# One decoder layer on one core: scores' matrix laid out batch by batch, fillers in the early gaps, all instruction orders rewritten

## The reference, cut to what matters

```
x = layernorm(x + attn(x));  x = layernorm(x + xattn(x, ctx));  x = layernorm(x + ffn(x))

attn:  q, k = elu(x Wq + bq) + 1, elu(x Wk + bk) + 1;  v = x Wv + bv        (16 heads of 8)
       k = k / sqrt(sum(k*k) + 1e-6);  out = (q k^T) v per head, then Wo
       a layernorm of x + out, times gamma, plus beta
xattn: q = x Wq, k = ctx Wk, v = ctx Wv   (16 heads of 64);  softmax(q k^T / 8) v, then Wo
ffn:   fp4_linear(x, w) = quant_dequant(x) @ quant_dequant(w)^T
       h = silu(fp4_linear(x, gate)) * fp4_linear(x, up);  fp4_linear(h, down)
       quant_dequant: blocks of 16, scale = max|x|/6, nearest value of 0, .5, 1, 1.5, 2, 3, 4, 6
```

## Time and profile before

| what | us |
|---|---|
| median of 3 runs | 360.56 |
| the profiled execution: its own time | 362.69 |
| the profiled execution: its span | 360.9 |
| TensorE busy | 342.2 (95%) |
| VectorE busy | 307.8 (85%) |
| GpSimd busy | 271.8 (75%) |
| ScalarE busy | 256.0 (71%) |

### The profile page before, as it was taken

One profiled execution on the slowest core, in us unless ns is written; L12 is line 12 of the kernel. 1 busy time (PEld: TensorE's weight loads), 2 busy tenths in 40 slices (PEclk: granted clock), 3 DMA queues, 4 the chain that ended last, 5 costly groups with the idle time before them and its releaser, 6 DMA issues.

```text
span 360.9 us, 7621 instructions
## 1 busy us (share of the span) xinstructions
PE 342.2 (95%) x2319; PEld 288.1 (80%) x2319; DVE 307.8 (85%) x851; ACT 256.0 (71%) x533; POOL 271.8 (75%) x453
## 2 busy tenths in 40 slices
PE   6789999999999999999999999999999999989884
PEld 6588858787779979977799977888897888968763
DVE  1599986667799998988889988989999987999994
ACT  2678886776788685797857677877877767666543
POOL 3275779889978769798777578979979897794445
PEclk9899999999999999999999999999999999999999
DMA  7821100000100000111001000001000000001001
GB/s 233 290 62 31 39 8 16 0 16 2 46 29 2 1 2 0 45 32 31 0 2 40 7 1 17 15 3 29 2 1 17 1 16 15 4 15 31 0 23 37
DMA packets 13587, 10.46 MB, mean 29 GB/s; under 512 B 971, under 2 KB 12396, under 8 KB 13548
## 3 DMA queue, kind: packets, MB, share of 16 engines
q1 hardware_dynamic: 12540, 7.89, 7.2%
q10 hardware_dynamic: 1008, 2.10, 1.6%
HBM read 7.88 MB, written 2.10 MB: 28 GB/s over the span
## 4 chain that ended last, share of the span: by engine, by line
PE 52%; POOL 16%; issue 14%; DVE 11%; ACT 4%; DMA 1%; POOLq 0%; ACTq 0%; DVEq 0%
PE A L2880 11%; PE S L2850 8%; PE TP L2837 5%; PE TP L2868 5%; PE F L2904 4%; POOL pe L445 3%; PE A L2798 3%; PE A L2924 2%; PE S L2859 2%; POOL fold L439 2%; PE TP L2776 2%; POOL hv L455 2%; DVE smax L1838 2%; PE TP L2913 2%; DMA wqkT<-in_wk_t 1%
## 5 line engine op out<-in xcount | busy, mean ns | idle before, releaser
L445 POOL TENSOR_TENSOR pe<-pe,srec 128x1024 f32<-128x1024 f32 x32 | 60.8, 1905 | 5.0 <-DVE srec L1855 4.9
L2880 PEld LDWEIGHTS A<-wvoT,wqkT 128*128 128x128 f32 x480 | 56.1, 192 | 2.0 <-issue 1.2
L2880 PE MATMUL A<-wvoT,wqkT 128*128 128x128 f32 x480 | 57.3, 275 | 0.0
L2850 PE MATMUL S<-M,x1T 128*128 128x512 f32 x192 | 52.8, 410 | 0.7 <-DVE x1T L1737 0.7
L439 POOL TENSOR_TENSOR fold<-pe 128x512 f32<-128x512 f32 x32 | 42.1, 1314 | 12.6 <-ACT pe L1081 12.4
L2850 PEld LDWEIGHTS S<-M,x1T 128*128 128x128 f32 x192 | 34.0, 189 | 10.4 <-issue 1.8
L1838 DVE TENSOR_REDUCE smax<-S 128x16 fp32r<-128x1024 f32 x32 | 38.9, 1215 | 2.2 <-PE S L2850 2.2
L1086 ACT ACTIVATE wqkT<-TP 128x1024 f32<-128x1024 f32 x32 | 32.7, 1021 | 10.9 <-PE TP L2868 10.8
L1081 ACT ACTIVATE pe<-S 128x1024 f32<-128x1024 f32 x32 | 32.6, 1018 | 5.8 <-PE S L2859 5.6
L2868 PE MATMUL TP<-ident,pe 128*128 128x128 f32 x256 | 33.6, 274 | 0.5 <-ACT wqkT L1086 0.2
L2904 PE MATMUL F<-w_gu_r,xf_r 128*128 128x352 f32 x168 | 33.9, 337 | 0.1
(11 more groups left out here) (246 smaller groups left out, 914.6 us busy)
## 6 DMA issues: line engine op xcount, KB each, us to landing
xT<-in_x_t SPq DMA_DIRECT2D x16, 128.0 KB, 2.2
x_sb<-in_x SPq DMA_DIRECT2D x16, 128.0 KB, 2.2
out<-yf SPq DMA_DIRECT2D x15, 128.0 KB, 1.8
pe<-in_fw SPq DMA_DIRECT2D x1, 560.0 KB, 10.6
wqkT<-in_wq_t ACTq DMA_DIRECT2D x2, 256.0 KB, 4.8
wqkT<-in_wk_t ACTq DMA_DIRECT2D x2, 256.0 KB, 6.3
ctx_f<-in_ctx_t ACTq DMA_DIRECT2D x2, 256.0 KB, 7.4
wvoT<-in_wv_t ACTq DMA_DIRECT2D x1, 512.0 KB, 8.9
```

The lines of the kernel that those rows point to most:

```text
L445: ge.tensor_tensor(w, w, spread(srec[n % NFO][:, :], HX, R), ALU.mult).then_inc(pn_made, 1)
L2850: last = te.matmul(S[:, half * BANK:half * BANK + BANK], part(x1T[b % 2][:, left, :], t), M[:, g % 2, right, HC * half:HC * half + HC, b % ...
L2880: last = te.matmul(part(A2, t), pT[n % 2][:, j, :], vo[b % 2][:, j, :], start=(j == 0 and b not in SUM_ON_PE), stop=(j == NJ - 1))
```

## The change

1. M becomes `[P, 2, 2, BG, HX, R]`: what `scores` reads is one run of 512 columns. ACT and DVE now read PSUM in runs of 64 columns (`m_by_batch`) and write four runs of 256.
2. Fillers: 5 before `g_product(0)`, 5 before `project_kv(1)`, 4 before `project_q(0)`, 4 before `kv_outer(0)`. Near the end 38 in nine places, where there were 24 in four.
3. The order of the calls is another one on all five engines. Functions and numbers of calls are the same.

```diff
-        M = sb("M", [P, 2, 2, HX, BG * R], FP32R)
+        M = sb("M", [P, 2, 2, BG, HX, R], FP32R)
+        def m_by_batch(g, q):
+            return M_BANKS[NQ * g + q][:, :].rearrange("p (h b r) -> p b h r", h=QH, b=BG)
         def m_part(g, q, part):
-            return M[:, g % 2, part, QH * q:QH * q + QH, :]
+            return M[:, g % 2, part, :, QH * q:QH * q + QH, :]
-                sc.activation(m_part(g, q, 0), m_bank(g, q), ACT.Copy).then_inc(m_high, 1)
+                sc.activation(m_part(g, q, 0), m_by_batch(g, q), ACT.Copy).then_inc(m_high, 1)
-                ve.tensor_tensor(m_part(g, q, 1), m_bank(g, q), m_part(g, q, 0).bitcast(FP32), ALU.subtract).then_inc(m_low, 1)
+                ve.tensor_tensor(m_part(g, q, 1), m_by_batch(g, q), m_part(g, q, 0).bitcast(FP32), ALU.subtract).then_inc(m_low, 1)
                     for half in range(2):
-                                         M[:, g % 2, right, HC * half:HC * half + HC, b % BG * R:b % BG * R + R],
+                                         M[:, g % 2, right, b % BG, HC * half:HC * half + HC, :],
...
             pe.wait_ge(const_made, 5)
+            keep_warm(A2, 5)
             g_product(0)
             project_kv(0)
             pe.wait_ge(fk_made, 1)
+            keep_warm(S0, 5)
             project_kv(1)
             g_product(1)
             pe.wait_ge(fk_made, 2)
+            keep_warm(S0, 4)
             project_q(0)
             pe.wait_ge(ky_made, 3)
+            keep_warm(S0, 4)
             kv_outer(0)
             kv_project(0)
             pe.wait_ge(fq_made, 1)
-            project_q(1)
+            project_kv(2)
             attn_out(0)
...
             project_kv(4)
-            pe.wait_ge(m_low, 5)
-            m_product(1, 3)
-            pe.wait_ge(m_low, 7)
-            x1_transpose(0)
-            pe.wait_ge(m_low, 6)
-            hw_product(1)
-            pe.wait_ge(fk_made, 5)
-            project_q(4)
             scores(0, 0)
             values(0)
+            pe.wait_ge(fk_made, 5)
+            project_q(4)
             scores_shift(0, 0)
-            pe.wait_ge(ky_made, 15)
-            kv_outer(3)
-            pe.wait_ge(fq_made, 5)
-            project_kv(5)
-            pe.wait_ge(pe_made, 1)
-            x1_transpose(1)
-            kv_project(3)
             pe.wait_ge(vo_kept, 1)
             values(1)
+            pe.wait_ge(pe_made, 1)
+            x1_transpose(1)
+            pe.wait_ge(m_low, 8)
+            weights_transpose(0)
+            pe.wait_ge(m_low, 8)
+            weights_transpose(1)
             pe.wait_ge(x1T_low, 2)
             scores(0, 1)
...
             xf_transpose(13)
             pe.wait_ge(hT_kept, 12)
+            pe.wait_ge(hT_kept, 12)
+            keep_warm(TP0, 8)
             p_transpose(15, 0)
...
             pe.wait_ge(yf_made, 13)
-            keep_warm(A2, 4)
+            pe.wait_ge(hg4_made, 14)
+            keep_warm(S0, 4)
+            down(13)
+            pe.wait_ge(yf_made, 14)
+            pe.wait_ge(hg4_made, 14)
+            keep_warm(S0, 2)
             tile_xf_transpose(15, 0)
-            pe.wait_ge(xfT_kept, 16)
-            down(13)
             pe.wait_ge(hg4_made, 15)
+            pe.wait_ge(hg4_made, 14)
+            keep_warm(S0, 5)
             tile_gate_up(15, 0)
```

More of the change, by code:

```diff
@@ L545, in _ @@
             shift_of("post", 0)
+            x_plus_rows(2)
+            k_norm(2)
+            minus_mean("attn", 1)
+            variance_eps("attn", 1)
+            rstd_of("attn", 1)
+            shift_of("attn", 1)
+            context_low(1)
             times_gamma(1)
@@ new lines, in _ @@
+            variance_eps("post", 8)
+            rstd_of("post", 8)
+            shift_of("post", 8)
+            k_norm(10)
+            variance_eps("attn", 9)
+            x_plus_rows(10)
+            minus_mean("ffn", 2)
+            minus_mean("attn", 9)
+            rstd_of("attn", 9)
+            shift_of("attn", 9)
+            h_dequantise(3)
+            times_gamma(9)
+            plus_x_beta(9)
+            fold_halves(7, 1)
+            probabilities(7, 0)
+            x_dequantise(5)
@@ L2067, in _ @@
+            k_miss(2, 1)
             aggregate("attn", 1)
[L2068 to L2071 removed]
             q_features(2)
             k_better(2, 1)
[L2074 removed]
             m_keep_low(1, 0)
+            m_keep_low(1, 1)
             keep_kvT(2)
[L2077 removed]
+            m_keep_low(1, 2)
             q_features(3)
+            weights_rounded_up()
             k_sums(3)
+            x1T_keep_low(0)
@@ L2370, in _ @@
+            xf_keep_low(5)
+            gated(4, 1)
+            h_max(4)
+            m_keep_low(3, 2)
+            score_reciprocals(7, 1)
+            ffn_residual(3)
+            score_max(8, 1)
+            score_sums(8, 0)
+            attn_residual(10)
+            statistics("attn", 10)
+            h_reciprocal(4)
+            x_max(6)
+            x_reciprocal(6)
+            h_scaled(4)
+            aggregate("attn", 10)
             statistics("ffn", 3)
-            aggregate("ffn", 3)
@@ L2586, in _ @@
+            score_sums(13, 0)
+            score_sums(13, 1)
+            score_reciprocals(13, 0)
+            score_reciprocals(13, 1)
+            statistics("cross", 12)
+            x_max(11)
+            aggregate("cross", 12)
+            x1T_keep_low(14)
+            gate_times(10, 0)
             attn_residual(15)
+            gated(10, 0)
             statistics("attn", 15)
             aggregate("attn", 15)
-            h_rounded_up(9)
-            h_rounded(9)
-            x_max(11)
+            score_max(14, 0)
@@ L2987, in _ @@
             m_product(0, 0)
-            pe.wait_ge(fq_made, 2)
-            project_kv(2)
             m_product(0, 1)
+            pe.wait_ge(fk_made, 3)
+            project_q(1)
             m_product(0, 2)
@@ L3116, in _ @@
             project_q(6)
-            pe.wait_ge(h_made, 1)
-            gate_up(0, 1)
-            pe.wait_ge(vo_kept, 5)
-            m_product(2, 0)
+            pe.wait_ge(pT_kept, 6)
+            values(4)
             pe.wait_ge(ky_made, 24)
```

2100 lines of the change are left out of this document (1029 added, 1071 removed).

## The result

The changed kernel takes 361.86 us (median of 7 executions, 361.46 to 362.25), the kernel before beside it 360.69 (7 executions). The ratio is 1.0027, interval 1.0017 to 1.0037: 1.2 us slower, where 1.2 us faster was forecast.

What follows compares the result with a forecast made beforehand. TensorE's work was taken to bind 71% of the span, with VectorE beside it early and VectorE alone in the tail. Terms +1.2 - 2.4 - 0.7 + 0.7 = -1.2 us took the 360.56 us median to 359.4, range 356.8 to 362.5.

Steps and rivals of the forecast that it cites:

- M batch by batch: nothing.: Scores' matmul: reading one run of 512 columns instead of runs of 64 gains nothing; at best 2.9 us less.
- Fillers at the start: +1.2 us.: Start, up to `m_product(0, 0)`: the added fillers lengthen the chain by 1.2 us; bounds 0 and +2.8.
- if the clock now holds: Start, at `project_kv(1)` and `g_product(1)`: full clock wins back 1.6 us, so `project_kv(1)` ends only 0.3 late.
- if the clock falls all the same: Start, upper bound +2.8 us: 5 fillers cost twice their time and the 1.6 us are not won.
- The offset: The sum: profiled execution 362.69 us becomes 361.5; the median is 2.13 lower, 360.56, so 359.4 us is predicted.
- Orders between 19.35 and 54: -2.4 us.: Up to 54 us: moved weights' steps and `k_norm(1)` win 2.4 of TensorE's 2.74 us idle time; bounds 2.74 and 0.
- Orders between 54 and 310: -0.7 us.: The middle: new orders win half of TensorE's 1.41 us idle time; bounds -1.41 and +1.4.
- The tail: +0.7 us.: Near the end: fillers before `tile_gate_up(15, 0)` and `tile_xf_transpose(15, 0)` cost 0.7 us, between 0 and 1.7.
- Slower: fillers behind their waits: Rival, at 11.7, 15.8 and 344 us: fillers behind waits lengthen the chain, 4.5 against 2.4 us; 362.7 us, chance 0.24.

Runs made afterwards that it cites:

- b_layout: The kernel before with nothing but M's layout changed: 360.84 us, ratio 0.9999 to the kernel before.
- a_no_start: The changed kernel without its 18 fillers at the start: 360.62 us, ratio 1.0000 to the kernel before.
- b_start: The kernel before with only the 18 start fillers added, behind their waits: 362.85 us, ratio 1.0057 to the kernel before.
- b_same: The kernel before, unchanged, run and profiled a second time: 360.73 us, ratio 1.0003.
- u_weights: New orders, fillers ahead of their waits, none before `g_product(0)` (357.87 us), with `weights_scaled` and `weights_rounded_up` put back to their old places: 361.48 us.
- f_wru: The kernel before with `weights_rounded_up` moved on VectorE to behind `x1T_keep_low(0)`: 361.47 us, ratio 1.0019 to the kernel before.
- f_dve2: As f_wru, with `weights_scaled` also moved, to behind `keep_kvT(1)`: 362.36 us, ratio 1.0041 to the kernel before.
- a_no_tail7: The changed kernel without the 7 fillers before `tile_xf_transpose(15, 0)` and `tile_gate_up(15, 0)`: 360.22 us, ratio 0.9986 to the kernel before.
- c_start_ahead: As a_no_tail7, with the fillers before `project_kv(1)`, `project_q(0)` and `kv_outer(0)` ahead of their waits: 360.97 us, ratio 0.9990 to the kernel before.
- c_none7: The changed kernel without the 18 start fillers and without the tail's 7: 360.74 us, ratio 0.9977 to the kernel before.

## Why the prediction was wrong, step by step

- **M batch by batch: nothing.** Right: 393 ns against 394, and b_layout at 0.9999.
- **Fillers at the start: +1.2 us.** This is the step that failed. Measured: 1.03 us to `project_kv(0)` and 1.52 behind it, 2.55 in all (after against a_no_start), and 2.0 in the old orders (b_start). The step had the parts right that follow their waits. It credited 1.6 us for "if the clock now holds", read from the earlier trace rows, and called the 5 before `g_product(0)` hidden behind the start at 9.11. In b_same `project_kv(0)` starts at 8.26 with no gap, so nothing hides them. The fall of the clock is common in the kernel before, but it costs far less than 1.6 us: 0.74 to `scores(8, 0)` in the execution of the forecast, 0.13 where it came at 16.4 us in b_layout, and nothing in the medians of the 120 executions. Low clock made single calls longer there; that the chain to the scores got longer by as much was taken without a reason. The 2.8 us that stood as the bound "if the clock falls all the same" is what came, without a fall.
- **The offset.** The sum was made against an execution of 362.69 us and carried over by a constant 2.13. But 1.6 of these were the late start of `project_kv(0)` and the 0.74 us behind it, the very things that the start's step had the fillers cure. The gain was booked against a median in which it had no place. That alone turns -1.2 into +0.4.
- **Orders between 19.35 and 54: -2.4 us.** The size was larger: -3.38 to `scores(8, 0)` (a_no_start against b_same), and the first scores came at 40.83 us, not at 42 to 43. That is more than the bound of 2.74, all the idle time from 19.35 to 54. Only 1.03 of the 3.38 is idle time; the step had no term for a shorter busy time of TensorE. The two steps did get short in their new places, and putting two steps of the weights back costs 3.6 us (u_weights), in which the shared port makes VectorE 1.1 us later. But in the old lists the same moves lose (f_wru, f_dve2). So each list is fitted to itself, and which share of the gain is the weights' steps' stays open.
- **Orders between 54 and 310: -0.7 us.** Nothing: 254.59 busy in both, and +0.38 from `scores(8, 0)` to the last `gate_up`, within the bounds.
- **The tail: +0.7 us.** Too small: 1.18 in the profile, in the upper half of its bounds. The busy VectorE covered none of the 5.
- **Rivals.** "Slower: fillers behind their waits" is the one that came true, with 2.55 + 1.18 = 3.7 us of its 4.5, against 3.4 - 0.4 = 3.0 brought by the orders in the profiles. It had a chance of 0.24. What spoke for it stood in the forecast's own rows: a profiled execution 2.1 us above the median of the others can't be typical in all its parts.

Left open: why the clock falls in some executions of a kernel and not in others, why it holds in a_no_tail7's tail and falls in c_start_ahead's with the same idle stretches, and why TensorE's busy time is shorter in the new order.

## What to carry to other kernels

Put a filler ahead of the wait in whose gap it is to run, never between the wait and the call that it frees: moving the same fillers from behind to ahead gained 1.41 us in the new orders, and 13 of them cost 1.06 us behind and nothing ahead in the old ones. They are worth having only where the clock falls without them. Don't read a single call's longer time at half clock as a loss of the whole. Before crediting an edit with curing something that the profile shows, see whether the profiled execution's own time is that of the others, and take a second profile if it isn't. The waits of the engine that binds show where an order can gain, but its idle time is no upper bound, and a step moved alone may only move the wait.

## What the runs showed of the hardware

- The clock rose to full at 4.29 to 7.67 us after the span's start, at another time in nearly every profiled execution. The clock of one kernel falls in some executions and not in others (c_none7: mean clock 0.984 to 0.999; the kernel before: 0.991 to 1.000).
- What a stretch at half costs hangs on its place: 0.13 us at 16.4 us in the old order, where TensorE had slack (169.34 against 169.21, b_layout and b_same), 1.6 us at 16.75 in the new one (167.46 against 165.83), 1.3 us in c_none7's tail (25.51 against 24.25) and 1.66 in a_no_start's.
